# Two transformer layers in exact fp32: layer 1's buffers laid over layer 0's, and the end of one layer merged with the start of the next

## The reference

```python
x = x + _layernorm(attn(_layernorm(x)))      # layer 0: 16 heads of 16, rope, causal softmax, biases
x = x + _layernorm(ffn(_layernorm(x)))       # layer 0: down(silu(gate(x)) * up(x)), 768 hidden, int weights / 127
# layer 1: 16 heads of 64
sim = jnp.einsum('bhid,bhjd->bhij', q, k) * SCALE
sim = SOFTCLAMP * jnp.tanh(sim / SOFTCLAMP)  # then causal softmax, times v, times Wo
# layer 1, feed-forward: xr, xk = mixes of x and x shifted by one token
r = jax.nn.sigmoid(jnp.einsum('btc,dc->btd', xr, W_r))
k_act = jnp.square(jax.nn.relu(jnp.einsum('btc,dc->btd', xk, W_k)))
out = r * jnp.einsum('btc,dc->btd', k_act, W_v)
```

## Time and profile before

| | |
|---|---|
| median of three runs | 1717.33 us |
| the profiled execution's own time, its span | 1717.42 us, 1715.6 us |
| TensorE busy | 1542.9 us, 90% of the span |
| VectorE, ACT, GpSimd busy | 1055.4 (62%), 832.0 (48%), 808.5 us (47%) |
| mean granted clock of TensorE | 0.939 of 2.4 GHz |
| DMA | 61.31 MB moved, 36 GB/s on average |
| layer 0's steady rounds | 90 to 91 us each |
| the stretch between the layers | 765 to 873 us |
| layer 1's steady rounds | 102.7 us each |

### The profile page before, as it was taken

The page is one execution under the profiler, slowest core; times in us unless marked ns, Lnnn a source line. Parts: engine busy times, 40 slices in busy tenths (PEclk is TensorE's granted clock), DMA queues, the critical chain, the costliest instruction groups (busy, mean ns, idle before and its releaser), DMA issues.

```text
span 1715.6 us, 28419 instructions
## 1 busy us (share of the span) xinstructions
PE 1542.9 (90%) x10528; PEld 1101.1 (64%) x10528; DVE 1055.4 (62%) x1802; ACT 832.0 (48%) x1211; POOL 808.5 (47%) x943
## 2 busy tenths in 40 slices
...
GB/s 147 60 51 50 50 63 50 63 50 52 47 52 44 54 45 43 48 6 130 44 1 25 1 14 25 1 38 1 13 24 12 24 0 24 12 1 25 1 25 13
DMA packets 46864, 61.31 MB, mean 36 GB/s; under 512 B 5024, under 2 KB 32064, under 8 KB 46784
## 3 DMA queue, kind: packets, MB, share of 16 engines
...
...
## 4 chain that ended last, share of the span: by engine, by line
PE 82%; DVE 6%; ACT 5%; POOL 3%; issue 2%; DMA 1%; SPq 0%; ACTq 0%; POOLq 0%; DVEq 0%
PE psum L293 41%; PE psum L1470 8%; PE psum L1447 7%; PE psum L1485 5%; PE psum L903 5%; PE psum L889 4%; PE psum L1458 4%; PE psum L861 3%; PE psum L865 2%; ACT l_probs L1258 2%; ACT l_probs L668 2%; DVE l_rowmax L730 1%; PE psum L923 1%; PE psum L873 1%; DMA l_qT<-l_roped_hi 1%
## 5 line engine op out<-in xcount | busy, mean ns | idle before, releaser
L668 ACT ACTIVATE l_probs<-psum 128x512 f32<-128x512 f32 (+1 forms) x384 | 180.9, 524 | 243.3 <-PE psum L889 243.2
L1339 DVE RECIPROCAL l_att<-psum 128x512 f32<-128x512 f32 x64 | 214.5, 3352 | 125.8 <-PE psum L1458 119.1
L730 DVE TENSOR_REDUCE l_rowmax<-psum 128x2 f32<-128x1024 f32 (+3 forms) x256 | 201.5, 818 | 53.8 <-PE psum L865 52.0
L1258 ACT ACTIVATE l_probs<-psum 128x1024 f32<-128x1024 f32 (+1 forms) x192 | 164.1, 880 | 101.1 <-PE psum L1447 79.1
L198 POOL TENSOR_TENSOR l_pool_holder<-expo 128x1 f32<-128x1 f32 x128 | 29.0, 226 | 333.7 <-ACT l_probs L668 205.3
L203 POOL TENSOR_SCALAR_AFFINE_SELECT l_probs<-l_probs 128x512 f32<-128x512 f32 (+1 forms) x320 | 165.2, 545 | 0.0
L1264 ACT ACTIVATE l_probs<-l_probs 128x2048 f32<-128x2048 f32 (+1 forms) x128 | 159.3, 1266 | 0.6
L1330 DVE TENSOR_TENSOR l_qk_lo<-psum,l_qk_hi 128x1024 fp32r<-128x1024 f32 x64 | 77.7, 1221 | 128.5 <-ACT l_qk_hi L1250 128.5
L1470 PE MATMUL psum<-l_probs,l_v 128*64 128x512 f32 (+3 forms) x1024 | 151.1, 437 | 0.0
L1209 POOL TENSOR_TENSOR l_attT_lo<-l_att,l_attT_hi 128x512 fp32r<-128x512 f32 x64 | 82.4, 1287 | 104.9 <-ACT l_attT_hi L1274 104.9
L1470 PEld LDWEIGHTS psum<-l_probs,l_v 128*64 128x64 f32 x1024 | 71.8, 138 | 92.9 <-issue 83.7
...
## 6 DMA issues: line engine op xcount, KB each, us to landing
...
l_xin<-in_x SPq DMA_DIRECT2D x8, 512.0 KB, 7.4
...
l_x<-in_x SPq DMA_DIRECT2D x8, 512.0 KB, 4.0
x_mid<-l_x SPq DMA_DIRECT2D x8, 512.0 KB, 3.0
l_xin<-x_mid SPq DMA_DIRECT2D x8, 512.0 KB, 3.9
```

The costliest lines, as they stand in the source:

```text
L668: ring_s.free(nc.scalar.activation(probs[:, SLOT[p], e, c0:c1], ring_s.unit(*use)[:, 0:c1 - c0], ACT.Exp, scale=HD0 ** -0.5), *use)
L730: reduced = nc.vector.tensor_reduce(rowmax[:, t, a // 2, :, a % 2], ring_d.unit("max", a, k)[:, :, c0:c0 + (t + 1) * P], mybir.AxisListTyp ...
L1258: ring_s.free(nc.scalar.activation(probs[:, p % 2, :, c0:c1], ring_s.unit("score", p, u)[:, :, 0:c1 - c0], ACT.Tanh, scale=HD1 ** -0.5 / C ...
L1339: ring_d.free(nc.vector.reciprocal(att[p % 2][:], ring_d.unit("den", p)), "den", p)
```

## The change

Five things are changed, in both layers.

1. Memory. Layer 1's early buffers (x, its transposes, wv, wq, wk, qk, probs, v, key sums, att) are laid on the left side of SBUF over layer 0's attention buffers, and wo, wrkv and the feed-forward buffers on the right side over layer 0's feed-forward buffers. `Ended` gives, for each buffer of layer 0, the wait after which it is free.
2. Weights. `Raw` takes the place of `Weights` for layer 1: ten pieces, each loaded straight to where its low part will be, and split there. wv is loaded after layer 0's last rope, wq after its last placement, wk after its last score, wo after its last up, wrkv after its last down. PE's and SP's `ready` are gone; a product of image 0 waits for the number of split pieces that it needs.
3. Order between the layers. Layer 0's last rounds and layer 1's first ones are sorted into one order, by times that `offset` and `closing_table` give.
4. The tables of both layers, of layer 0's start too, have new times.
5. Layer 1's probs of a pair are packed in 1280 columns a head, so that its mask is three selects of POOL instead of two.

```diff
--- before.py
+++ after.py
-UNITS1 = ((0,), (1, 3), (2,))
-OFF1 = (0, 512, 1024, 896)
+UNITS1 = ((0,), (3, 1), (2,))
+OFF1 = (0, 640, 1024, 512)
 ROWS1 = 1280
-STEP1 = 1536
...
+class Raw:
+
+
+    def __init__(self, nc, sem, plan):
+        self.nc, self.plan = nc, plan
+        self.loaded = [sem(f"w_loaded{n}") for n in range(len(plan))]
+        self.high_done, self.low_done = sem("w_hi"), sem("w_lo")
+
+    def load(self, sp, n):
+        src, _, _, raw, free = self.plan[n]
+        free(sp)
+        sp.dma_start(raw, src).then_inc(self.loaded[n], 16)
+
+    def high(self, act, n):
+        _, hi, _, raw, _ = self.plan[n]
+        act.wait_ge(self.loaded[n], 16)
+        self.nc.scalar.activation(hi, raw, ACT.Copy).then_inc(self.high_done, 1)
+
+    def low(self, dve, n):
+        _, hi, lo, raw, _ = self.plan[n]
+        dve.wait_ge(self.high_done, n + 1)
+        self.nc.vector.tensor_tensor(lo, raw, hi.bitcast(F32), ALU.subtract).then_inc(self.low_done, 1)
+
+    def split(self, pe, i, count):
+        if isinstance(i, int) and i == 0:
+            pe.wait_ge(self.low_done, count)
...
-        "rope_hi": {(0,): -7.32, (1,): -2.13, (2,): 5.19, (3,): 7.23},
+        "rope_hi": {(0,): -2.55, (1,): -0.93, (2,): 1.88, (3,): 7.67},
-        "place": {(0,): 3.12, (1,): 7.3, (2,): 12.31, (3,): 21.51},
+        "place": {(0,): -2.61, (1,): -2.24, (2,): 8.88, (3,): 10.62},
...
+    end = BATCH - 1
+    ended = Ended(
+        roped=lambda eng: ring_d.filled(eng, end, "rope", ROPES - 1),
+        projected=lambda eng: ring_s.filled(eng, end, "v", 1),
+        placed=placed_all,
+        scored=lambda eng: ring_s.filled(eng, end, "score", PAIRS - 1, len(PAIR_UNITS) - 1, 1),
+        weighted=lambda eng: ring_d.filled(eng, end, "pv", 3),
+        attended=lambda eng: ring_d.freed(eng, end, "outT", 3),
+        score_freed=lambda eng: ring_s.freed(eng, end, "score", PAIRS - 1, len(PAIR_UNITS) - 1, 1),
+        x1_ready=lambda eng: eng.wait_ge(x1_ready.sem, x1_ready.at(BATCH, 0)),
+        up_done=lambda eng: ring_e.filled(eng, end, "up", NM - 1),
+        down_done=lambda eng: ring_e.filled(eng, end, "down", 2),
+        down_freed=lambda eng: ring_e.freed(eng, end, "down", 2),
+        stored=lambda eng: eng.wait_ge(x_stored.sem, x_stored.at(BATCH, 0)))
+    return schedule.tail(SLOTS), tail_pieces, ended
...
+    def split_weight(name, shape, side):
+
+        place = memory.enter_context
+        hi = place(nc.sbuf_tensor(f"l1_{name}_hi", shape, F32R, side=side))
+        with nc.sbuf_tensor(f"l1_{name}_raw", shape, F32, side=side) as raw:
+            pass
+        return hi, place(nc.sbuf_tensor(f"l1_{name}_lo", shape, F32R, side=side)), raw
+
+    wv = split_weight("wv", [P, NC, F1], "left")
     xin = sb("xin", [P, NT, D])
     xT = [sb("xT" + s, [P, NC, T], F32R) for s in ("_hi", "_lo")]
-
-
-    qk1 = [sbr("qk" + s, [P, 2, 2, T], F32R) for s in ("_hi", "_lo")]
-    v1 = sbr("v1", [P, NT, H1, HD1])
+    att = [sb(f"att{k}", [P, T]) for k in range(2)]
+    wq = split_weight("wq", [P, NC, F1], "left")
+    wk = split_weight("wk", [P, NC, F1], "left")
+    qk1 = [sb("qk" + s, [P, 2, 2, T], F32R) for s in ("_hi", "_lo")]
+    probs = sb("probs", [P, 2, 2, ROWS1])
+    v1 = sb("v1", [P, NT, H1, HD1])
+    keysum = sb("keysum", [P, 2, 2, T - P])
...
+        "load": {(0,): 220.97, (1,): 221.47, (2,): 221.97, (3,): 222.47, (4,): 232.57, (5,): 237.37, (6,): 253.827, (7,): 257.256, (8,): 260.684, (9,): 264.113},
+        "high": {(0,): 192.23, (1,): 192.73, (2,): 195.445, (3,): 195.9, (4,): 200.347, (5,): 200.793, (6,): 245.327, (7,): 245.683, (8,): 248.25, (9,): 248.575},
+        "low": {(0,): 193.633, (1,): 194.037, (2,): 194.665, (3,): 222.39, (4,): 230.541, (5,): 230.926, (6,): 245.34, (7,): 245.39, (8,): 250.41, (9,): 250.835},
...
+    offset = 233.82
+    closing_table = {
+        "o": {(0, 7): 236.647, (1, 7): 236.673},
+        "x1_T": {(0, 7): 240.317, (1, 7): 240.323},
...
         own = tail_pieces[eng.engine]
-        for _, (name, *k), b in sorted(tail_order + [(time, piece, None) for piece, time in prologue.items()], key=lambda entry: entry[0]):
-            if b is None and name in pieces:
-                pieces[name](*(() if name in ("small", "high", "low", "constants") else (0,)), *k)
-            elif b is not None and name in own and (name, b) != ("store", BATCH - 1):
-                own[name](b, *k)
-        if "ready" in pieces:
-            pieces["ready"]()
-        for j in range(schedule.last + 1):
+        merged = [(closing.get((*piece, b), time), own, piece, b) for time, piece, b in tail_order]
+        merged += [(time, pieces, piece, None) for piece, time in prologue.items()]
+        merged += [(offset + j * SLOTS + schedule.place[piece], pieces, piece, j - schedule.shift[piece])
+                   for j in range(schedule.first, lo) for piece in schedule.order if schedule.present(j, piece)]
+        for _, table, (name, *which), b in sorted(merged, key=lambda entry: entry[0]):
+            if name in table:
+                table[name](*(() if b is None else (b,)), *which)
+        for j in range(lo, schedule.last + 1):
             if j == lo:
                 with eng.Fori(lo, hi + 1) as i:
                     schedule.iteration(i, pieces)
-            elif not lo < j <= hi:
+            elif j > hi:
...
-            flat = probs[:, p % 2, :, :].rearrange("p e c -> p (e c)")
-            mask_heads(nc, flat.rearrange("p (n q) -> p n q", q=BANK)[:, :, 0:P], masked)
-            mask_heads(nc, rows[:, :, OFF1[3]:OFF1[3] + P], masked)
+            mask_heads(nc, rows.rearrange("p e c -> p (e c)").rearrange("p (n q) -> p n q", q=OFF1[1])[:, :, 0:P], masked)
+            for kt in (3, 2):
+                mask_heads(nc, rows[:, :, OFF1[kt]:OFF1[kt] + P], masked)
...
-    for name, dst in (("wv1", wv), ("wq1", wq), ("wk1", wk), ("wrkv", wrkv)):
-        for c in range(NC):
-            plan.append((a[name][c * P:(c + 1) * P, :], dst[0][:, c, :], dst[1][:, c, :], False))
-    for c in range(NP1):
-        plan.append((a["wo1"][c * P:(c + 1) * P, :], wo[0][:, c, :], wo[1][:, c, :], False))
-    weights = Weights(nc, sem, plan, staging)
+    rows = lambda w: w.rearrange("(c p) d -> p c d", p=P)
+    for name, dst, before in (("wv1", wv, ended.roped), ("wq1", wq, ended.placed), ("wk1", wk, ended.scored),
+                              ("wo1", wo, ended.up_done), ("wrkv", wrkv, ended.down_done)):
+        half = dst[0].shape[1] // 2
+        for c in (slice(0, half), slice(half, 2 * half)):
+            plan.append((rows(a[name])[:, c, :], dst[0][:, c, :], dst[1][:, c, :], dst[2][:, c, :], before))
+    weights = Raw(nc, sem, plan)
...
-        def attended():
-
-            tail_pieces[sp.engine]["attended"]()
-            sp.dma_start(xin[:], tok(x_mid, 0)).then_inc(x_loaded.sem, 16)
-            for n in range(len(plan)):
-                weights.load(sp, n)
-            tail_pieces[sp.engine]["store"](BATCH - 1)
-            tail_pieces[sp.engine]["stored"]()
-
         def load_x(i):
             if started(i):
                 ring_d.filled(sp, i - 1, "x_T", NT // 2 - 1)
-                sp.dma_start(xin[:], tok(x_mid, i)).then_inc(x_loaded.sem, 16)
+            else:
+                ended.projected(sp)
+            sp.dma_start(xin[:], tok(x_mid, i)).then_inc(x_loaded.sem, 16)
...
-            pe.wait_ge(weights.low_done, len(plan))
-
         def x_T(i, b):
             ring_d.claim(pe, i, "x_T", b)
+            if not started(i):
+                ended.attended(pe)
...
             ring_s.claim(pe, i, "qk", p)
-            for b, w in enumerate((wq, wk)):
+            if not started(i):
+                ended.score_freed(pe)
+            weights.split(pe, i, 6)
```

More of the change, by code:

```diff
@@ L169, in claim @@
                 pe.wait_ge(self.empty[freer], self.count(it, last, self.group(last)))
+@dataclass
+class Ended:
+    roped: object
+    projected: object
+    placed: object
+    scored: object
+    weighted: object
+    attended: object
+    score_freed: object
+    x1_ready: object
+    up_done: object
+    down_done: object
+    down_freed: object
+    stored: object
 PAIR_UNITS = ((0,), (3, 1), (2,))
@@ L435, in phase1 @@
+        "hidden_lo": {(0,): 42.8, (1,): 46.81, (2,): 48.18, (3,): 48.59, (4,): 50.83, (5,): 52.55},
+        "down": {(0,): 54.57, (1,): 55.71, (2,): 56.23, (3,): 56.43},
+        "x2_stats": {(): 55.03},
+        "x2_rstd": {(): 56.76},
+        "x2_norm": {(): 56.15},
+        "x2": {(): 58.28},
+        "store": {(): 61.73},
     }
@@ L574, in _ @@
                      "residual": residual})
-        tail_pieces[sp.engine]["attended"] = lambda: ring_d.filled(sp, BATCH - 1, "outT", 3)
-        tail_pieces[sp.engine]["stored"] = lambda: sp.wait_ge(x_stored.sem, x_stored.at(BATCH, 0))
     @block.gpsimd
@@ L1086, in program @@
+    closing = {(name, *which): time for name, entries in closing_table.items() for which, time in entries.items()}
     def program(eng, pieces):
```

(9 more changed lines are left out.)

364 lines of the change are left out of this document (193 added, 171 removed).

## The result

The changed kernel takes 1739.22 us (median of 4, 1738.15 to 1740.87) against 1717.54 of the kernel before: ratio 1.013, 95% interval 1.0112 to 1.0147. The forecast was 1698, in a range of 1679 to 1715. It was on the wrong side.

The account below looks back on a forecast made before the run. TensorE was taken as the bound, with 82% of the chain, so only its idle or half-clock time counts. Boundary -23, layer 0's rounds +3.5, start +1, tail -0.7: -19.2 us on 1717.42, giving 1698, range 1679 to 1715.

Parts of the forecast that it names:

- The boundary: From layer 0's last products to layer 1's fifth qk product: of 39.9 us lost, 17.2 stay, so 23 us gained.
- the 2 us put ahead of the window: Before 765.2 us: splits of wv and wq queued on ACT and VectorE between exp 5 and gated 5, costing 2 us.
- the 39.9: Loss at the boundary in the kernel before: 31.6 us of TensorE idle plus 8.3 us to the low clock.
- Layer 0's rounds: Later rope placement idles TensorE 1.5 us a round, shorter v to pv 0 gives 1.0 back: +3.5 us over 7 rounds.
- A + 6.4: Layer 0: the placement's first transfer starts 6.4 us after score 3,2 on TensorE (A), 2.4 us later than before.
- the slack: Layer 0: time between the rope placement's landing and the max product that needs it, put at 1.0 us.
- rival 1: Layer 0: the late placement's idle also starts a second half-clock dip in each of 7 rounds, +25 us, 1723; chance 0.08.
- -1.0 a round for v to pv 0: Layer 0: TensorE's idle stretch from v to pv 0 gets 1.0 us shorter each round through the new order.
- Layer 1's rounds: Full, waiting 1.2 us a round; the third mask select adds 0.13 us on GpSimd, covered by TensorE work: no change.
- The start: Second placement no longer behind a weight fetch (-0.9), image 1's rope splits later (+2): +1 us, between -1 and +3.
- The last part of layer 1: GpSimd's last rstd leaves the last image's chain (-1.0), two masks cost 0.13 more each: -0.7 us.
- The rule on the shared port: Boundary: VectorE splits and GpSimd operations exclude each other whole, up to 13 us; the prediction took 0.3 each, under 1.

Follow-up runs that it names:

- a_rope: Changed kernel with layer 0's rope high parts 0 and 1 back at their earlier place on ACT and hidden_lo 0 behind rope_lo 1 on GpSimd: 1712.4 us.
- a_both: Changed kernel with the edits of a_qkhi and a_rope together: 1674.6 us, ratio 0.9752 to the kernel before.
- a_qkhi: Changed kernel with pair 6's qk high part in layer 1 made on ACT ahead of the sigmoid of r: 1699.0 us.
- a_wk: a_both with wk's two low parts on VectorE moved behind outT_norm 3 of the last image: 1676.1 us.

## Why the prediction was wrong, step by step

- **The boundary** was right in mechanism and close in size. The walk had the attention transposes 2.0 us later (measured 1.7: 795.63 - 788.14 = 7.5 from the statistics on, before 768.77 - 762.93 = 5.8), a wait for qk_lo 1 of 1.3 (1.5), for hidden_lo 5 of 1.9 (1.8), the 11.3 us wait filled whole. The statistics before:

```profile
762.93 1.42 DVE l_x_stats L269 x4
```

In its own window it gave 28.1 us (107.80 - 79.67) against 24.7 (22.7, and the 2 us put ahead of the window). What was to stay in the window, 15.2 us, was 15.0: 10.1 idle and 4.9 of clock. But the clock fell elsewhere than the walk had it: not in qk 0, which ran at full clock (800.69 on), but from 813.4 us on, where 3.1 us were lost and the walk had 2 us without a row. And the loss before was larger than the 39.9 worked out: some of the down products ran at half clock too, 1.7 us. The windows, after and before:

```profile
813.40:820.20 6.80, 6.18 (x25) 4.99 (x26) 4.11 (x15) 5.22 (x6) 1.11 (x2) 0.50 0.00 0
815.90:819.30 3.40, 3.40 (x17) 3.40 (x18) 3.40 (x4) 3.30 (x7) 0.00 (x0) 0.50 0.24 62
```

The 2 us ahead of the window did not come (+0.2 in that stage).
- **Layer 0's rounds** are the first failing step. "1.5 us idle in each of 7 rounds" was 2.1. The walk was right up to the placement's start (A + 6.4) and the product's turn (A + 19.4). The failed term is the slack: 12.8 us of bytes and an estimated 1.6 gave 1.0 us, while the twelve transfers take 14.9 from the first start to the last landing, so 0.3 was left. The late second group, which the walk did not follow, would have given the same wait alone, but added nothing to it. Larger than this was the clock behind the wait (3 to 7 us at half clock, so 1.7 to 3.4 us lost). It was rival 1's with a chance of 0.08; it came in 5 of 6 rounds. The argument against it, that the stretch there is dense, did not hold: one wait in a dense stretch was enough. And the -1.0 a round for v to pv 0 did not come: a_rope's rounds are the old length. Sum: +3.7 for +0.5.
- **Layer 1's rounds** are the second, and as large a miss: "These are full and wait 1.2 us a round ... nothing". The new table was not walked through for its PSUM ring there; key behind qk 6 behind the sigmoid gives 3.3 us of waiting by durations that the trace of before had (1.0 for either step on ACT, 1.2 for qk_lo). Without it the same rounds are 1.4 us shorter than before, so the step missed +5.2 and -1.4. Why they are shorter, beyond 1.0 us less of waiting, was not tried.
- **The start** was +4.4 for +1; 2.4 of it stay in a_both, and their cause was not tried.
- **The last part of layer 1** went from 83.1 to 84.8 us in its last round and not by -0.7; a_qkhi has it at 79.0, so the same wait was in it. The -0.7 itself was not tried alone.
- **The rule on the shared port.** The prediction took 0.3 us a split from the earlier trace rows. The changed kernel's splits on VectorE beside GpSimd's key sums (min/median/max ns), and then the late wo splits of the kernel before:

```profile
L290 DVE TENSOR_TENSOR l_wo_lo<-l_wo_raw,l_wo_hi x2: 1755/1762/1770, 863.9 to 865.5; 128x1024 fp32r<-128x1024 f32 x2
L290 DVE TENSOR_TENSOR l_wrkv_lo<-l_wrkv_raw,l_wrkv_hi x2: 959/1668/2376, 883.3 to 886.0; 128x768 fp32r<-128x768 f32 x2
```

```profile
L246 DVE TENSOR_TENSOR l_wo_lo<-l_probs,l_wo_hi x8: 408/410/1960, 819.5 to 834.6; 128x256 fp32r<-128x256 f32 x8
```

The 1024-wide one was 1.21 alone, the 768-wide one is 0.96 at best. The second wrkv split took 2.38, so it stood still for 1.4 us beside key sums of 1.8. The trace of before had it too: one wo split took 1.96 us where the others took 0.41, beside a GpSimd addition of 2.39 us. And the split of the earlier trace rows was no weaker case: it began at 807.43, GpSimd's operation ended at 807.88, and the split 1.1 us after that. That is what the Trainium skill ("SBUF — State Buffer", section "SBUF: two separate sides") says, whole or nearly whole; 0.3 us was the part of an operation that was left, and not the price. No wait of TensorE in the changed kernel names a split, and of the splits only wk's, at 1.2 us each, are on its chain from 784 to 875 us, so the time was hardly touched; in a_wk 1.8 us of it reached TensorE.
